# Group-norm variance on DVE behind its copy of the group sums, instead of on GpSimd

## The chip, the cores and the metric

One core of a Trainium2 chip. Time is device microseconds of one execution; a kernel's time is the median of its runs. The profile is one further execution, with the hardware profiler on. Engines: TensorE (PE; PEld is its weight load), VectorE (DVE), ScalarE (ACT), GpSimd (POOL), and SP, which issues the DMAs of the loop.

## The reference

The input is x of shape (64, 256, 14, 14), fp32. Four layers follow one another, each on all 256 channels of 196 tokens:

- L0: batch norm, depthwise 3x3 and pointwise convolution to q, k, v; k and v resized to 7x7; attention with a position bias; depthwise and pointwise convolution; residual; batch norm, relu and a 256x256 product, residual.
- L1: group norm (8 groups), linear attention with softmax over k's channels and q's tokens, projection, plus the normalised input.
- L2: group norm (32 groups), attention with 8 heads, projection, residual.
- L3: group norm (32 groups), attention with one head, projection, residual.

The part that the change touches is the group norm of L1, L2 and L3:

```python
mean = xg.mean(axis=(2, 3, 4), keepdims=True)
var = xg.var(axis=(2, 3, 4), keepdims=True)
xg = (xg - mean) * rsqrt(var + EPS)
x = xg.reshape(B, C, H, W)
return x * gamma + beta
```

## The kernel before, in words

The 64 images are worked on in 32 pairs. Channels lie on the partitions (2 blocks of 128), the tokens of both images (2 x 196) on the free axis. All weights stay on the chip.

The work of a pair is spread over several turns of one software pipeline. Each engine has a table (`PE_AT`, `ACT_AT`, `DVE_AT`, `POOL_AT`, `SP_AT`) that gives each step a start in slots, and 128 slots are one turn: slot modulo 128 is the place in the turn, slot divided by 128 says how many turns after the pair's first one the step runs. `step(t)` walks the 128 slots and issues what stands there; `run` unrolls the first and the last turns and loops over the others. So in one turn the order on each engine is fixed by its table, and steps of up to seven pairs alternate in it. Every engine's queue is worked off in that order; between engines counted semaphores (`Count`) are waited for. PSUM banks are shared by several steps in a fixed order: `full` waits until TensorE has filled a bank for a step, `free` until the steps before it have read theirs, `read` until that step has been read.

A group norm n (1, 2, 3) of a pair goes like this:

- DVE, `stats{n}`: `group_stats` takes bn_stats of 4 blocks (channel block x image), aggregates, and adds mean squared to the variance (lines 933 to 946).
- TensorE, `gn{n}`: one small product with a block matrix spreads each group's mean and mean of squares over its channels, into 8 columns of a bank (line 1414).
- DVE, `gn{n}`: copies these 8 columns to `group` in SBUF (line 1008). Ahead of it stands a wait for GpSimd's steps of the pair before.
- GpSimd, `gn{n}`: `normalized` (lines 568 to 588) works out mean squared, variance, the clamp at zero plus EPS, the power -0.5, scale, and shift, seven linked instructions of 128x4, and then applies scale and shift to the four blocks of the tile (line 587).
- ScalarE, `high{n}_c`, rounds the tile to a high part, DVE, `low{n}_c`, takes the rest as a low part (lines 781 and 1093); the products of the layer use both.

`linker` makes one instruction wait for the one before it on the same engine:

```python
def link(ins):
    done[0] += 1
    ins.then_inc(count.sem, 1)
    eng.wait_ge(count.sem, count.at(p, done[0]))
```

In one turn DVE meets the copies in the order gn2 (slot 6), gn1 (slot 45), gn3 (slot 92), each for another pair. What stands behind each copy on DVE:

- gn1: four taps of the first depthwise convolution (line 1140), then the row maximum of a head group of L2 (`nm`, line 958), which ScalarE's exponentials (line 822) need; further taps; the reciprocal of the row sums (`rden`, line 1063), which ScalarE's scaling of the heads (line 830) needs; TensorE then transposes each scaled head (line 1222). Later comes the sum of L2's projection (line 1079).
- gn2: the low part of an attention result (line 1069), low parts, the sums of L3's output `o3_1` and `o3_0` out of PSUM (line 1121), first taps and the residual sum `pw1` (line 989). `o3_0` frees bank c, which TensorE's scores of L0 (`s0_0`) fill next.
- gn3: reciprocals `rk` (line 1026) and `r` (line 1113, L3's row sums; ScalarE's line 877 needs it), the sum and maximum of `kv`, taps of the second depthwise convolution (line 1159), the maximum of another head group, and at last the residual sum `pw0` (line 989).

Of the kernel before, what the change touches and what calls it, by code (L numbers as in the profile page):

```python
# [10 lines left out]
ALU = mybir.AluOpType  # L11
# [11 lines left out]
EPS = 1e-5  # L23
# [104 lines left out]
def build(nc, a):  # L128
    ctx = ExitStack()
    with ctx:  # L130
        def sb(name, shape, dt=F32):
            return ctx.enter_context(nc.sbuf_tensor(name, shape, dt))
# [4 lines left out]
        class Count:  # L137


            def __init__(self, name, per):  # L140
                self.sem, self.per = sem(name), per
# [119 lines left out]
        class GroupNorm:  # L261


            def __init__(self, n):
                self.stats = sb(f"gn{n}_stats", [128, 4, 6])
                self.mine = sb(f"gn{n}_mine", [128, 2, 4])
                self.sq = sb(f"gn{n}_sq", [128, 4])
                self.group = sb(f"gn{n}_group", [128, 2, 4])
                self.v = sb(f"gn{n}_v", [128, 4])
                self.y = sb(f"gn{n}_y", [128, 4])  # L270
                self.t = sb(f"gn{n}_t", [128, 4])
                self.scale = sb(f"gn{n}_scale", [128, 4])
                self.shift = sb(f"gn{n}_shift", [128, 4])
                self.stat_steps = Count(f"gn{n}_stat_steps", 9)
                self.stats_ready = Count(f"gn{n}_stats_ready", 1)
                self.steps = Count(f"gn{n}_steps", 4 + 3)
                self.done = Count(f"gn{n}_done", 4)
                self.high = Count(f"gn{n}_high", KC)
                self.low = Count(f"gn{n}_low", KC)

        gn = {1: GroupNorm(1), 2: GroupNorm(2), 3: GroupNorm(3)}
# [15 lines left out]
        def tile(use):  # L297
            return home[use].t
# [4 lines left out]
        def emptied(use):  # L303
            return home[use].emptied

        def full(p, use):

            return home[use].filled, home[use].fills(p, use)
# [5 lines left out]
        def read(p, use):  # L314

            return home[use].emptied, home[use].reads(p, use, 1)
# [13 lines left out]
        def ends(*uses):  # L330

            return [use for use in uses if use == latest(*(o for o in uses if home[o] is home[use]))]
# [54 lines left out]
        def pair_of(t, u, start):  # L387

            if start % SLOTS != u:
                return None  # L390
            p = t - start // SLOTS
            return p if not isinstance(t, int) or 0 <= p < PAIRS else None

        def linker(eng, count, p, k):

            done = [k]
# [5 lines that stand above are left out]
            return link  # L402
# [9 lines left out]
        def of_image(i):  # L412
            return slice(i * TOK, (i + 1) * TOK)
# [118 lines left out]
        def _(pool):  # L532
            g = nc.gpsimd
# [7 lines left out]
            def alone():  # L541

                pool.sem_inc(pool_held, 1)
# [24 lines left out]
            def normalized(p, n, src, dst):  # L568

                t = gn[n]  # L570
                weight, bias = w[f"gn{n}_w"], w[f"gn{n}_b"]
                link = linker(pool, t.steps, p, 0)
                pool.wait_ge(*read(p, f"gn{n}"))
                pool.wait_ge(t.done.sem, t.done.at(p, 0))
                link(g.tensor_tensor(t.t[:], t.group[:, 0], t.group[:, 0], ALU.mult))  # L575
                link(g.tensor_tensor(t.v[:], t.group[:, 1], t.t[:], ALU.subtract))
                alone()
                link(g.tensor_scalar(t.v[:], t.v[:], 0.0, EPS, ALU.max, ALU.add))
                link(g.tensor_tensor(t.y[:], t.v[:], minus_half[:], ALU.pow))
                link(g.tensor_tensor(t.scale[:], t.y[:], weight[:], ALU.mult))  # L580
                link(g.tensor_tensor(t.t[:], t.group[:, 0], t.scale[:], ALU.mult))  # L581
                link(g.tensor_tensor(t.shift[:], bias[:], t.t[:], ALU.subtract))  # L582
                for c in range(KC):
                    for i in range(2):
                        j = 2 * c + i
                        alone()
                        g.tensor_scalar(dst[:, c, of_image(i)], src[:, c, of_image(i)], t.scale[:, j:j + 1],  # L587
                                        t.shift[:, j:j + 1], ALU.mult, ALU.add).then_inc(t.done.sem, 1)

            def step(t):  # L590
                for u in range(SLOTS):
# [25 lines left out]
                    if p is not None:  # L617
                        if is_first(p):
                            pool.wait_ge(weights_in, WEIGHTS)
                        if has_before(p):  # L620
                            for use in ends("out0", "out1"):
                                pool.wait_ge(*read(p - 1, use))
                        normalized(p, 1, x1, xn1)
                    p = pair_of(t, u, POOL_AT["gn2"])
                    if p is not None:
                        pool.wait_ge(gn[2].low.sem, gn[2].low.at(p, 0))
                        normalized(p, 2, x2, xn2)
# [261 lines left out]
        def _(dve):  # L889
            v = nc.vector  # L890
# [42 lines left out]
            def group_stats(p, n, src):  # L933
# [11 lines left out]
                link(v.tensor_tensor(t.sq[:], t.mine[:, 0], t.mine[:, 0], ALU.mult))  # L945
                v.tensor_tensor(t.mine[:, 1], t.mine[:, 1], t.sq[:], ALU.add).then_inc(t.stats_ready.sem, 1)

            def step(t):
                for u in range(SLOTS):

                    for g in range(GROUPS):
                        for m in range(2):
                            p = pair_of(t, u, DVE_AT[f"max{g}_{m}"])
# [8 lines left out]
                    for i in range(2):  # L962
                        use = f"s0_{i}"
                        p = pair_of(t, u, DVE_AT[use])
                        if p is not None:
# [5 lines left out]
                            link = linker(dve, l0_soft_steps[i], p, 0)  # L971
# [3 lines left out]
                        p = pair_of(t, u, DVE_AT[f"sum0_{i}"])  # L975
                        if p is not None:
                            dve.wait_ge(l0_exp_done.sem, l0_exp_done.at(p, i + 1))
                            dve.wait_ge(l0_probs.sem, l0_probs.at(p, 0))
                            link = linker(dve, l0_soft_steps[i], p, 2)
                            link(v.tensor_reduce(out=d0[:, i], in_=s0[:, i], axis=AX.X, op=ALU.add))  # L980
                            v.reciprocal(r0[:, i], d0[:, i]).then_inc(l0_soft_steps[i].sem, 1)  # L981
                    for c in range(KC):
                        use = f"pw{c}"
                        p = pair_of(t, u, DVE_AT[use])
# [5 lines left out]
                        use = f"mlp{c}"  # L990
                        p = pair_of(t, u, DVE_AT[use])
# [5 lines left out]
                    for n, src, last in ((1, x1, "mlp"), (2, x2, "out"), (3, x3, "proj")):  # L997
                        p = pair_of(t, u, DVE_AT[f"stats{n}"])
                        if p is not None:
                            for use in ends(f"{last}0", f"{last}1"):  # L1000
                                dve.wait_ge(*read(p, use))
                            group_stats(p, n, src)
                        use = f"gn{n}"
                        p = pair_of(t, u, DVE_AT[use])
                        if p is not None:
                            dve.wait_ge(*full(p, use))
                            dve.wait_ge(gn[n].steps.sem, gn[n].steps.at(p, 0))
                            v.tensor_copy(gn[n].group[:], tile(use)[:, 0:8].rearrange("p (a b) -> p a b", a=2)  # L1008
                                          ).then_inc(emptied(use), 1)

                    for j in range(4):
                        use = f"kv{j}"
                        p = pair_of(t, u, DVE_AT[use])
# [8 lines left out]
                        p = pair_of(t, u, DVE_AT[f"rk{j}"])  # L1022
# [4 lines left out]
                    for c in range(KC):  # L1027
                        use = f"q1_{c}"
                        p = pair_of(t, u, DVE_AT[use])
                        if p is not None:  # L1030

                            dve.wait_ge(*full(p, use))
                            link = linker(dve, q_less_steps, p, 2 * c)
# [4 lines left out]
                        p = pair_of(t, u, DVE_AT[f"rq{c}"])  # L1038
# [6 lines left out]
                    for c in range(KC):  # L1045
                        use = f"out{c}"
                        p = pair_of(t, u, DVE_AT[use])
# [7 lines left out]
                    for g in range(GROUPS):  # L1055
                        i = g // 2
                        for m in range(2):
                            p = pair_of(t, u, DVE_AT[f"rden{g}_{m}"])
# [6 lines left out]
                        use = f"av{g}"  # L1065
                        p = pair_of(t, u, DVE_AT[use])
# [4 lines left out]
                    for c in range(KC):  # L1071
                        use = f"proj{c}"
                        p = pair_of(t, u, DVE_AT[use])
# [8 lines left out]
                    for c in range(KC):  # L1082
                        p = pair_of(t, u, DVE_AT[f"act0_low{c}"])
# [3 lines left out]
                    for n, src, dst, _ in splits:  # L1087
                        for c in range(KC):
                            p = pair_of(t, u, DVE_AT[f"low{n}_{c}"])
# [5 lines left out]
                    for i in range(2):  # L1095
                        use = f"s3_{i}"
                        p = pair_of(t, u, DVE_AT[use])
                        if p is not None:
# [4 lines left out]
                            link = linker(dve, l3_less_steps, p, 3 * i)  # L1103
# [5 lines left out]
                        p = pair_of(t, u, DVE_AT[f"r3_{i}"])  # L1109
# [4 lines left out]
                    for i in range(2):  # L1114
                        use = f"o3_{i}"
                        p = pair_of(t, u, DVE_AT[use])
# [8 lines left out]
                    for k in range(9):  # L1125
                        p = pair_of(t, u, DVE_AT[f"conv1_{k}"])
# [17 lines left out]
                    for k in range(9):  # L1144
                        p = pair_of(t, u, DVE_AT[f"conv2_{k}"])
# [411 lines left out]
```

## Time and profile before

| what | us |
|---|---|
| median of 3 runs | 2110.89 (2110.83 to 2111.57) |
| the profiled execution, whole | 2112.12 |
| its span, first to last instruction | 2109.7 |
| TensorE busy | 2011.4 (95%), 15232 matmuls |
| TensorE weight loads busy | 1689.6 (80%) |
| ScalarE busy | 1886.4 (89%) |
| DVE busy | 1843.0 (87%) |
| GpSimd busy | 973.3 (46%) |
| DMA | 70.31 MB, mean 33 GB/s |

The mean granted TensorE clock is 0.980; it is 1.00 from 188 us on until the last 85 us. Busy times are sums of the records of an engine; records of neighbouring instructions overlap a little. A row of the timeline gives start, duration, engine, line, operation, tile written and tiles read, count where neighbouring ones are merged, and in brackets how long the engine sat idle before it and which instruction ended that. A row of the groups gives count, busy time, mean of one in ns, and the idle time before them. A row of the windows gives, for a stretch, its length and each engine's busy time with its number of instructions. Idle time of an engine that is not the bottleneck costs nothing.

### The profile page before, as it was taken

The page shows a single profiled execution, that of the slowest core. Times are in us where ns is not written, and L with a number is a line of the kernel's source. Part 1 is how long each engine was busy: PE and PEld are TensorE (multiplying, and loading weights), DVE is VectorE, ACT ScalarE, POOL GpSimd, SP SyncE. Part 2 cuts the span into 40 slices and gives each one's busy share as a digit, 9 for nine tenths or more (in the row PEclk, how much of TensorE's full clock was granted, in tenths as well). Part 3 has the DMA queues.
Part 4 walks back from the last instruction along what each step waited for, and adds up shares of the span by engine and source line. Part 5 has one row for each costly group of instructions (what it writes and reads, how often), then busy time and mean ns, then how long its engine had stood idle before and what let it go on. Part 6 is the DMA issues. An engine that isn't in the chain of part 4 may idle for free.

```text
span 2109.7 us, 57712 instructions
## 1 busy us (share of the span) xinstructions
PE 2011.4 (95%) x15232; PEld 1689.6 (80%) x15232; DVE 1843.0 (87%) x4683; ACT 1886.4 (89%) x6231; POOL 973.3 (46%) x1707
## 2 busy tenths in 40 slices
PE   4589999999999999999999999999999999999977
PEld 3367888888888888888888888888888888888766
DVE  6789999999999999999999999999999999997532
ACT  2269999999999999999999999999999999999984
POOL 3544544545444454544445454444545544453211
PEclk8799999999999999999999999999999999999988
DMA  4000011001101100110111011011101101000000
GB/s 129 16 24 24 17 40 40 24 30 38 38 23 38 38 30 24 38 38 23 38 38 36 18 38 38 23 38 38 38 15 38 38 27 34 31 32 17 24 24 39
DMA packets 29819, 70.31 MB, mean 33 GB/s; under 512 B 6252, under 2 KB 7088, under 8 KB 29744
## 3 DMA queue, kind: packets, MB, share of 16 engines
q1 hardware_dynamic: 26928, 67.68, 9.1%
q10 hardware_dynamic: 2816, 1.72, 0.3%
q8 instruction: 36, 0.59, 0.1%
q14 instruction: 39, 0.32, 0.0%
HBM read 30.85 MB, written 12.85 MB: 21 GB/s over the span
## 4 chain that ended last, share of the span: by engine, by line
PE 88%; ACT 4%; DVE 1%; issue 1%; DVEq 0%; ACTq 0%
PE ps_e L1167 21%; PE ps_c L1167 21%; PE ps_b L1167 15%; PE ps_a L1167 11%; PE ps_s L1167 10%; PE ps_s L1222 8%; ACT e L830 1%; PE ps_a L1469 1%; ACT e L822 1%; ACT pt L836 0%; PE ps_e L1298 0%; PE ps_a L1298 0%; DVE nm L958 0%; ACT e L877 0%; ACT kv L742 0%
## 5 line engine op out<-in xcount | busy, mean ns | idle before, releaser
L822 ACT ACTIVATE e<-ps_s,nm 98x196 f32<-98x196 f32 x1024 | 423.9, 436 | 36.2 <-DVE nm L958 32.0
L830 ACT ACTIVATE e<-e,rden 98x196 f32<-98x196 f32 x1024 | 403.2, 462 | 0.2 <-DVE rden L1063 0.2
L1159 DVE SCALAR_TENSOR_TENSOR y<-opad,w_dw,y 128x406 f32<-128x406 f32 x512 | 314.9, 666 | 0.0
L1140 DVE SCALAR_TENSOR_TENSOR y<-xpad,w_dw,y 128x406 f32<-128x406 f32 x512 | 298.4, 636 | 0.0
L587 POOL TENSOR_SCALAR xn<-x,gn_scale,gn_shift 128x196 f32<-128x196 f32 x384 | 286.1, 757 | 20.8 <-POOL gn_shift L582 20.8
L575 POOL TENSOR_TENSOR gn_t<-gn_group 128x4 f32<-128x4 f32 x96 | 27.7, 289 | 563.7 <-DVE gn_group L1008 430.1
L958 DVE TENSOR_REDUCE nm<-ps_s 98x4 f32<-98x784 f32 x256 | 239.4, 966 | 34.2 <-PE ps_s L1167 34.2
L836 ACT COPY pt<-ps_s 98x392 f32<-98x392 f32 x512 | 233.3, 502 | 4.7 <-PE ps_s L1222 2.8
L1222 PE MATMUL ps_s<-w_eye,e 98*98 98x98 f32 x2048 | 228.9, 249 | 7.3 <-ACT e L830 7.2
L1222 PEld LDWEIGHTS ps_s<-w_eye,e 98*98 98x98 f32 x2048 | 200.5, 130 | 38.8 <-issue 22.3
L822 ACT ACTIVATION_READ_ACCUMULATOR e<-ps_s,nm 98x1 f32 x1024 | 222.7, 217 | 0.0
L599 POOL TENSOR_TENSOR p<-s,r 98x392 f32<-98x392 f32 x64 | 64.3, 1005 | 225.5 <-DVE r L981 225.5
L1167 PE MATMUL ps_c<-xs,ws_q 128*128 128x392 f32 x768 | 166.8, 352 | 0.0
L1167 PEld LDWEIGHTS ps_c<-xs,ws_q 128*128 128x128 f32 x768 | 133.0, 189 | 0.1
L1093 DVE TENSOR_TENSOR xs<-xn,xs 128x392 fp32r<-128x392 f32 x192 | 115.6, 603 | 16.8 <-ACT xs L781 15.4
L581 POOL TENSOR_TENSOR gn_t<-gn_group,gn_scale 128x4 f32<-128x4 f32 x96 | 123.3, 1285 | 7.5
L1167 PE MATMUL ps_s<-k,q 32*98 32x196 f32 x2048 | 118.6, 345 | 8.3 <-ACT q L791 2.3
L1167 PE MATMUL ps_s<-pt,v 98*32 98x196 f32 x2048 | 112.5, 337 | 6.8 <-ACT e L822 6.3
L1167 PEld LDWEIGHTS ps_s<-k,q 32*98 32x98 f32 x2048 | 77.4, 160 | 49.3 <-issue 28.0
L1167 PE MATMUL ps_a<-ws_v,xs 128*98 128x256 f32 (+1 forms) x768 | 112.3, 288 | 0.9 <-ACT opad L721 0.7
L1167 PEld LDWEIGHTS ps_a<-ws_v,xs 128*98 128x98 f32 x768 | 94.6, 163 | 21.6 <-issue 10.3
L939 DVE BATCH_NORM_STATS2 gn_stats<-x 128x6 f32<-128x196 f32 x384 | 109.7, 347 | 1.1
(223 smaller groups left out, 5326.6 us busy)
## 6 DMA issues: line engine op xcount, KB each, us to landing
x_in<-in_x SPq DMA_DIRECT2D x32, 392.0 KB, 3.2
x_res<-in_x SPq DMA_DIRECT2D x32, 392.0 KB, 3.1
x2b<-x SPq DMA_DIRECT2D x32, 392.0 KB, 2.7
out<-x SPq DMA_DIRECT2D x32, 392.0 KB, 2.6
out_pairs<-out SPq DMA_DIRECT2D x32, 392.0 KB, 2.5
w_q<-in_q SPq DMA_DIRECT2D x3, 256.0 KB
w_k<-in_k SPq DMA_DIRECT2D x3, 256.0 KB
w_v<-in_v SPq DMA_DIRECT2D x3, 256.0 KB
```

The lines of the kernel that those rows point to most:

```text
L581: link(g.tensor_tensor(t.t[:], t.group[:, 0], t.scale[:], ALU.mult))
L587: g.tensor_scalar(dst[:, c, of_image(i)], src[:, c, of_image(i)], t.scale[:, j:j + 1], t.shift[:, j:j + 1], ALU.mult, ALU.add).then_inc(t. ...
L822: s.activation(e2[:, j, tc], tile(use)[0:HALF, of_image(tc)], ACT.Exp, bias=nm2[:, j, tc:tc + 1], accum_out=den2[:, 2 * i + tc, h:h + 1]). ...
L830: s.activation(e2[:, j, tc], e2[:, j, tc], ACT.Copy, scale=rden2[:, 2 * i + tc, h:h + 1]).then_inc(p2_done[j].sem, 1)
L836: s.copy(turned(j), tile(use)[0:HALF, 0:N2]).then_inc(emptied(use), 1)
L939: v.bn_stats(t.stats[:, j], src[:, j // 2, of_image(j % 2)]).then_inc(t.stat_steps.sem, 1)
L958: v.tensor_reduce(out=nm2[:, two], in_=ps_s[0:HALF, two, 0:N2].rearrange("p b (c n) -> p b c n", c=2), axis=AX.X, op=ALU.max, negate=True) ...
L1093: v.tensor_tensor(dst[:, 1, c], src[:, c], dst[:, 0, c], ALU.subtract).then_inc(gn[n].low.sem, 1)
L1140: v.scalar_tensor_tensor(out=dst, in0=window(xpad, c, k, CR), scalar=tap, in1=dst, op0=ALU.mult, op1=ALU.add).then_inc(conv1_steps.sem, 1)
L1159: v.scalar_tensor_tensor(out=dst, in0=window(opad, c, k, CR), scalar=tap, in1=dst, op0=ALU.mult, op1=ALU.add).then_inc(conv2_steps.sem, 1)
L1167: return nc.tensor.matmul(dst, lhsT, rhs, start=start, stop=stop)
L1222: last = nc.tensor.transpose(tile(use)[0:HALF, of_tile(sc, tc)], e2[:, j, tc, sc * HALF:(sc + 1) * HALF], eye[0:HALF, 0:HALF])
```

## The change

Three of the seven small instructions of `normalized` go from GpSimd to DVE: mean squared, the subtraction, and the clamp with EPS. A new function `variance` on DVE issues the copy, waits for it, and issues the three, each linked to the one before by a new counter `var_steps`. Mean squared goes to `sq`, which the statistics use before. GpSimd waits for the third count of `var_steps` instead of for the copy, and starts with the power. Power, scale, shift and the four passes over the tile stay on GpSimd; the counter `steps` has four steps a pair instead of seven. The tables of slots stay as they are.

```diff
-                self.steps = Count(f"gn{n}_steps", 4 + 3)
+                self.steps = Count(f"gn{n}_steps", 1 + 3)
+                self.var_steps = Count(f"gn{n}_var_steps", 3)
...
-                pool.wait_ge(*read(p, f"gn{n}"))
+                pool.wait_ge(t.var_steps.sem, t.var_steps.at(p, 3))
                 pool.wait_ge(t.done.sem, t.done.at(p, 0))
-                link(g.tensor_tensor(t.t[:], t.group[:, 0], t.group[:, 0], ALU.mult))
-                link(g.tensor_tensor(t.v[:], t.group[:, 1], t.t[:], ALU.subtract))
-                alone()
-                link(g.tensor_scalar(t.v[:], t.v[:], 0.0, EPS, ALU.max, ALU.add))
                 link(g.tensor_tensor(t.y[:], t.v[:], minus_half[:], ALU.pow))
...
+            def variance(p, n, use):
+
+                t = gn[n]
+                link = linker(dve, t.var_steps, p, 0)
+                v.tensor_copy(t.group[:], tile(use)[:, 0:8].rearrange("p (a b) -> p a b", a=2)).then_inc(emptied(use), 1)
+                dve.wait_ge(*read(p, use))
+                link(v.tensor_tensor(t.sq[:], t.group[:, 0], t.group[:, 0], ALU.mult))
+                link(v.tensor_tensor(t.v[:], t.group[:, 1], t.sq[:], ALU.subtract))
+                v.tensor_scalar(t.v[:], t.v[:], 0.0, EPS, ALU.max, ALU.add).then_inc(t.var_steps.sem, 1)
...
                             dve.wait_ge(gn[n].steps.sem, gn[n].steps.at(p, 0))
-                            v.tensor_copy(gn[n].group[:], tile(use)[:, 0:8].rearrange("p (a b) -> p a b", a=2)
-                                          ).then_inc(emptied(use), 1)
+                            variance(p, n, use)
```

## Rows read from the trace of the kernel before

**Rows 1.** The page, chain that ended last, shares of the span by engine

```profile
PE 88%; ACT 4%; DVE 1%; issue 1%; DVEq 0%; ACTq 0%
```

**Rows 2.** Windows: us, busy of PE, PEld, DVE, ACT, POOL; clock, DMA, GB/s

```profile
257.00:318.50 61.50, 61.47 (x479) 51.96 (x476) 57.04 (x146) 58.72 (x197) 30.88 (x54) 1.00 0.10 35
318.50:1606.60 1288.10, 1285.60 (x9955) 1087.72 (x9956) 1200.60 (x3046) 1230.21 (x4076) 637.59 (x1114) 1.00 0.09 33
1606.60:1913.00 306.40, 305.90 (x2370) 258.94 (x2370) 279.40 (x715) 291.71 (x969) 149.71 (x269) 1.00 0.09 31
```

**Rows 3.** Groups of instructions by line and shape, GpSimd, whole span

```profile
L576 POOL TENSOR_TENSOR gn_v<-gn_group,gn_t 128x4 f32<-128x4 f32 x96 | 33.2, 345 | 7.5
L578 POOL TENSOR_SCALAR gn_v<-gn_v 128x4 f32<-128x4 f32 x96 | 28.3, 294 | 19.2 <-POOL gn_v L576 19.2
L575 POOL TENSOR_TENSOR gn_t<-gn_group 128x4 f32<-128x4 f32 x96 | 27.7, 289 | 563.7 <-DVE gn_group L1008 430.1 <-issue 133.7
```

**Rows 4.** Timeline of GpSimd, a first normalisation in the loop

```profile
1047.39 0.47 POOL L575 TENSOR_TENSOR gn_t<-gn_group 128x4 f32<-128x4 f32 x1 [0.81 <-DVE gn_group L1008]
...
1049.10 1.25 POOL L579 TENSOR_TENSOR gn_y<-gn_v,minus_half 128x4 f32<-128x4 f32 x1
```

**Rows 5.** Timeline of ScalarE, pair 0 and the last pair

```profile
95.23 0.52 ACT L781 CAST xs<-xn 128x392 fp32r<-128x392 f32 x1 [0.76 <-POOL xn L587]
...
2083.45 0.52 ACT L781 CAST xs<-xn 128x392 fp32r<-128x392 f32 x1 [1.81 <-POOL xn L587]
```

**Rows 6.** Timeline of DVE around a first normalisation in the loop

```profile
1045.60 0.16 DVE L945 TENSOR_TENSOR gn_sq<-gn_mine 128x4 f32<-128x4 f32 x1
1045.80 0.16 DVE L946 TENSOR_TENSOR gn_mine<-gn_mine,gn_sq 128x4 f32<-128x4 f32 x1
1047.06 0.17 DVE L1008 COPY gn_group<-ps_a 128x8 f32<-128x8 f32 x1 [1.09 <-PE ps_a L1167]
1047.15 2.30 DVE L1140 SCALAR_TENSOR_TENSOR y<-xpad,w_dw,y 128x406 f32<-128x406 f32 x4
1049.63 1.86 DVE L958 TENSOR_REDUCE nm<-ps_s 98x4 f32<-98x784 f32 x2 [0.17 <-PE ps_s L1167]
...
1055.78 0.17 DVE L1063 RECIPROCAL rden<-den 98x4 f32<-98x4 f32 x1
...
1060.90 0.63 DVE L1079 SCALAR_TENSOR_TENSOR x<-ps_e,pb,x2b 128x392 f32<-128x392 f32 x1 [0.23 <-PE ps_e L1167]
```

**Rows 7.** Timeline of DVE, behind a second normalisation in the loop

```profile
1032.12 0.74 DVE L1121 SCALAR_TENSOR_TENSOR out<-ps_c,ob,out 128x196 f32<-128x196 f32 x2
```

**Rows 8.** Groups of instructions by line and shape, DVE, whole span

```profile
L1036 DVE TENSOR_SCALAR bq_less<-nmq,w_qb 128x2 f32<-128x2 f32 x64 | 19.0, 297 | 2.3
...
L894 DVE TENSOR_SCALAR bn_half<-bn_v 128x4 f32<-128x4 f32 x1 | 0.2, 170 | 0.0
```

**Rows 9.** Timeline of ScalarE, scaling of the heads behind rows 6

```profile
1055.98 1.50 ACT L830 ACTIVATE e<-e,rden 98x196 f32<-98x196 f32 x4
...
1057.86 0.81 ACT L830 ACTIVATE e<-e,rden 98x196 f32<-98x196 f32 x2
```

**Rows 10.** Timeline of TensorE, the two steps that need these results

```profile
1033.50 0.93 PE L1167 MATMUL ps_c<-k,q 128*98 128x98 f32 x8
...
1058.74 0.84 PE L1222 MATMUL ps_s<-w_eye,e 98*98 98x98 f32 x8
```

**Rows 11.** Timeline of DVE, the wait ahead of the pointwise sum

```profile
1027.84 0.57 DVE L989 TENSOR_TENSOR x<-ps_c,x_res 128x392 f32<-128x392 f32 x1 [0.75 <-PE ps_c L1167]
```

**Rows 12.** Timeline of DVE, behind pair 1's first normalisation

```profile
137.56 1.85 DVE L958 TENSOR_REDUCE nm<-ps_s 98x4 f32<-98x784 f32 x2 [0.22 <-PE ps_s L1167]
```

**Rows 13.** Timeline of ScalarE, behind the first third-normalisation

```profile
224.07 0.42 ACT L822 ACTIVATE e<-ps_s,nm 98x196 f32<-98x196 f32 x1 [0.59 <-DVE nm L958]
...
227.98 0.32 ACT L843 CAST as<-ps_s 128x196 fp32r<-128x196 f32 x1 [0.18 <-PE ps_s L1167]
```

**Rows 14.** Timeline of ScalarE, behind the last third-normalisation

```profile
2079.31 0.81 ACT L877 ACTIVATE e<-e,r 98x196 f32<-98x196 f32 x2 [2.55 <-DVE r L1113]
```

## Prediction

> **What bounds the kernel now.** I read the chain that ended last first: it is TensorE for 88% of the span [rows 1]. The question is then how much TensorE idles where. The windows answer it: over 21 pairs of the loop (1288.10 us, so 61.34 us a pair) TensorE is busy 1285.60 us [rows 2]. It waits 0.12 us a pair. In the loop nothing that ends earlier on GpSimd or DVE can shorten the run; something that ends later on DVE can lengthen it. The stretches from 257 us and up to 1913 us are as full [rows 2], so TensorE fills (1913 - 257)/61.34 = 27 pairs. Ahead of them the pipeline fills and behind them it empties; there the engines wait for each other.
>
> **What leaves GpSimd.** Three instructions per normalisation, 96 of each: 27.7 + 33.2 + 28.3 = 89 us of busy time [rows 3]. On the path from DVE's copy to the power this is, in the first normalisation of a pair, 1047.39 to 1049.10 = 1.71 us [rows 4]. GpSimd is busy for half of the loop (637.59 of 1288.10 us) [rows 2], so the busy time itself is worth nothing; only the earlier end of the normalised tile could be, where someone waits for it. ScalarE shows such waits twice: 0.76 us for pair 0, 1.81 us for the last pair [rows 5].
>
> **What comes to DVE.** Three linked small instructions behind the copy, each started only when the one before has finished. The nearest row is the same pattern in the statistics: 1045.60 to 1045.80, 0.20 us from start to start with a record of 0.16 [rows 6]. Unlinked, the next instruction starts 0.09 us after the copy (1047.06 to 1047.15) [rows 6]. So copy to multiply 0.20, to subtract 0.20, to the tensor_scalar 0.20, and 0.09 to the next, against 0.09 before: everything behind the copy on DVE starts **0.60 us later**. The last instruction has immediate scalars; the kernel has one such of 0.170 us, and one with pointer scalars and fewer columns of 0.297 us [rows 8]. Bounds: below, 3 x 0.09 = 0.27 us if the waits cost nothing; above, 0.60 + 0.13 = 0.73 us if the tensor_scalar is as slow as the second. I take 0.60, since the 0.20 is the same operation, shape and link. GpSimd's power then starts 0.60 + 0.17 + 0.16 = 0.93 us after the copy instead of 2.04 (1047.06 to 1049.10).
>
> The Trainium skill (VectorE: DVE Perf Modes, section "The DRAIN you can't avoid") says that a semaphore after each of several chained DVE instructions costs nothing against one after the last. By it the sum would be +0.3 us instead of +2.0; the 0.20 against 0.09 us [rows 6] speaks against it.
>
> The wait on GpSimd moves from the copy to the third step; behind it on GpSimd's queue are the power, scale, shift and the four passes of the tile, and ScalarE's splits wait for those. The wait ahead of DVE's copy, for GpSimd's steps of the pair before, is about a pair old and free. No DMA is issued, moved or passed by.
>
> **Where 0.60 us on DVE goes in the loop**, normalisation by normalisation. "Slack" is the start of the waiting instruction minus the end of what it needs, less 0.03 us for the signal (rden ends 1055.95, ScalarE starts 1055.98) [rows 6, 9].
> - First (copy at 1047.06). Behind it are four taps, then a maximum that already waits 0.17 us for TensorE [rows 6]; records overlap by 0.08, so 0.25 is absorbed and 0.35 goes on to rden at 1055.78 and so to ScalarE at 1055.98. ScalarE's third head ends at 1057.86 + 0.81 = 1058.67 [rows 9]; its transposes are the second half of the eight from 1058.74 on (0.84 us), so they start at about 1058.74 + 0.42 = 1059.16, or 1059.08 where records overlap by the same 0.08 [rows 10]. Slack 0.38: it holds, by 0.03 us. What remains on DVE is taken up before the projection's sum, which waits 0.23 us for TensorE [rows 6].
> - Second. The last sum of o3_0 ends at 1032.12 + 0.74 = 1032.86 and frees the bank that TensorE writes from 1033.50 [rows 7, 10]: slack 0.61, and between copy and sum (some 4 us) DVE waits for nobody. 0.60 uses it up.
> - Third. Its hold-up ends at latest where DVE waits 0.75 us for the pointwise sum [rows 11]; I see no TensorE work that needs an earlier one of these within 0.2 us.
> Since two of three places are left with 0.01 to 0.03 us, I put 0.02 us a pair: 27 x 0.02 = 0.5 us.
>
> **At the edges** ScalarE and DVE set the pace, so a hold-up there is on the path. Pair 1's first normalisation stands before a maximum that waits 0.22 us [rows 12]: 0.60 - 0.30 = 0.30 us; pair 2's repeats it: 0.30. At the first third-normalisation DVE is behind: ScalarE waits 0.59 us for its maximum, and then has only a 0.18 us wait for TensorE to give back [rows 13]: 0.60 - 0.26 = 0.34. In the last third-normalisation the reciprocal r stands right behind the copy and ScalarE has waited 2.55 us for it [rows 14], with TensorE idle behind: 0.60. For pair 0 I count nothing: GpSimd is earlier, DVE later. Sum of the edges 1.54 us.
>
> **Sum**: 0.5 + 1.5 = +2.0 us. The profiled execution took 2112.12 us, so 2114.1; the median of the runs stands 1.2 us under it, 2110.89, so **2112.9 us**, +0.1%. About 0.2% (4.2 us) is what a measurement of this kernel can tell from no change.
>
> **Rivals.**
> 1. *A wait of TensorE in every pair* (slower). Place: the bank freed by o3_0's sum, and the third head's transposes. It decides from a hold-up of 0.61 us on. Price at 0.73: 0.12 + (0.48 - 0.38) = 0.22 us x 27 = 5.9 us, and edges 2 x 0.43 + 0.47 + 0.73 = 2.1: 2118.9 us. For: the slack is used up to the hundredth, and the ends of matmuls are modelled. Against: 0.20 a step is a measured pattern in the same loop. Chance 0.22.
> 2. *The links are free.* Each of the three steps takes 0.09 us, the hold-up is 0.27: nothing in the loop, at the edges 0 + 0 + 0.01 + 0.27: +0.3, 2111.2 us. For: the unlinked step of 0.09 us; against: the linked one of 0.20, both in one stretch [rows 6]. Chance 0.13. This is the case that the Trainium skill's section named above describes.
> 3. *The earlier tile pays* (faster). Each of ScalarE's two waits for GpSimd ends at most 2.04 - 0.93 = 1.1 us earlier: -2.2 us, 2108.7, if DVE's low halves and TensorE's older work didn't end last there. In the loop at most the 0.12 us a pair could go, -3.2 us. Only both together, 2105.5, pass 0.2%. Against: TensorE's loop is full without a wait for GpSimd. Chance 0.05.
> 4. *The change makes nothing of its own*: DVE's steps vanish in waits everywhere, 2110.9. Chance 0.04; the row of 2.55 us, with r right behind, speaks against it.
> The forecast keeps 0.56.
>
> **Numbers.** The forecast, rivals 2 and 4 and parts of 3 and 1 (hold-ups of 0.61 to 0.65 us) lie within 0.2%: 0.56 + 0.13 + 0.04 + 0.03 + 0.02 = 0.78. Slower: the other 0.20 of rival 1. Faster: the other 0.02 of rival 3. The range runs from 2110.0 (rival 4, less a microsecond of scatter) to 2118.0, which takes in rival 1 up to a hold-up of about 0.71 us; it leaves out rival 3 and the top of rival 1, together 0.15 or so.
>
> **What would show it.** Each step right: multiply, subtract and tensor_scalar on DVE at 0.20 us start to start, the next instruction 0.68 us after the copy; GpSimd's busy time down by some 89 us and DVE's up by 96 x 3 x 0.165 = 47 us; the power 0.93 us after the copy; TensorE's pair still 61.3 to 61.4 us; the maximum after the first normalisation without its 0.17 us wait; r at the end 0.60 us later. Wrong: a pair of 61.5 us or more, with new waits of TensorE for o3_0's sum or for ScalarE's scaling; or a last chain in which GpSimd's passes appear.

## The result, and the profile after

The changed kernel takes **2161.62 us** (median of 4 runs, 2160.23 to 2162.25), the kernel before 2110.86 beside it: ratio 1.0239 [1.0226, 1.0252], slower by 50.8 us. The forecast was 2112.9, its range ended at 2118.0. The profiled execution took 2160.23 us, its span is 2158.2 (2109.7 before).

The page of the changed kernel: its busy times, two of its DMA queues, and the chain that ended last.

```profile
PE 2030.6 (94%) x15232; PEld 1690.4 (78%) x15232; DVE 1885.1 (87%) x4971; ACT 1890.8 (88%) x6231; POOL 827.7 (38%) x1419
...
q14 instruction: 154, 1.26, 0.2%
q8 instruction: 37, 0.61, 0.1%
...
PE 58%; DVE 18%; issue 11%; ACT 5%; DVEq 2%; ACTq 0%
```

What was moved is there: DVE has 288 instructions and 42 us more (1843.0 before), GpSimd 146 us less (973.3 before). But the chain, TensorE's for 88% before [rows 1], is now DVE's for 18% and "issue" for 11%. And q14, a queue that carries instructions (an edit of DVE's program alone will move its packets below, so DVE's are among them), has 154 packets; before it had 39 (0.32 MB, so 8.2 KB each). From 450 to 1800 us, deep in the loop, it carried none before and 106 after. That is new work that stands in no term of the forecast.

The waits of DVE say where it hurts (us in total, times, longest):

```profile
DVE x L1058 <- issue: 42.3, 23, 2.0
```

The loop has 24 turns (t = 7 to 30), so it branches back 23 times. L1058 (L1052 before) is the projection's sum x2, whose two halves stand on either side of the branch. Before there is no idle time between them:

```profile
1023.93 0.62 DVE L1052 SCALAR_TENSOR_TENSOR x<-ps_e,w_pb,xn 128x392 f32<-128x392 f32 x1
1024.47 0.62 DVE L1052 SCALAR_TENSOR_TENSOR x<-ps_b,w_pb,xn 128x392 f32<-128x392 f32 x1
```

The changed kernel's DVE around the branch and behind a first normalisation, then GpSimd (start, us, operation, idle time before it and what ended that):

```profile
1043.83 0.62 DVE L1058 SCALAR_TENSOR_TENSOR x<-ps_e,w_pb,xn 128x392 f32<-128x392 f32 x1
1046.20 0.62 DVE L1058 SCALAR_TENSOR_TENSOR x<-ps_b,w_pb,xn 128x392 f32<-128x392 f32 x1 [1.75 <-issue]
...
1068.29 0.17 DVE L949 COPY gn_group<-ps_a 128x8 f32<-128x8 f32 x1 [1.22 <-PE ps_a L1173]
1068.49 0.16 DVE L951 TENSOR_TENSOR gn_sq<-gn_group 128x4 f32<-128x4 f32 x1
1068.69 0.16 DVE L952 TENSOR_TENSOR gn_v<-gn_group,gn_sq 128x4 f32<-128x4 f32 x1
1068.89 0.17 DVE L953 TENSOR_SCALAR gn_v<-gn_v 128x4 f32<-128x4 f32 x1
1068.98 2.29 DVE L1146 SCALAR_TENSOR_TENSOR y<-xpad,w_dw,y 128x406 f32<-128x406 f32 x4
...
1069.22 1.30 POOL L576 TENSOR_TENSOR gn_y<-gn_v,minus_half 128x4 f32<-128x4 f32 x1 [1.35 <-DVE gn_v L953]
```

The three new steps stand 0.20 us apart, as their model in [rows 6], the next instruction 0.69 us behind the copy, and the power 0.93 us behind it. What TensorE waits for from 413.4 to 1635.8 us, where nothing of the kind is listed for the kernel before:

```profile
PE ps_e L1173 <- DVE gn_mine L943: 17.2, 20, 1.0
PE ps_c L1173 <- DVE kv L1024: 5.2, 19, 0.3
PE ps_e L1173 <- DVE x L1085: 4.5, 19, 0.3
```

The window of that stretch (columns as in [rows 2]): TensorE is idle for 28.5 of 1222.4 us.

```profile
413.40:1635.80 1222.40, 1193.87 (x9153) 999.24 (x9153) 1127.31 (x2975) 1134.20 (x3738) 494.70 (x846) 1.00 0.09 33
```

The largest wait, 0.9 us a pair, stands right behind the gap: the group sums of the second normalisation need the statistics that DVE does after the branch. The period of a pair comes from two starts of the first normalisation's statistics, 22 pairs apart: (1825.81 - 431.68)/22 = **63.37 us**, against 61.34.

```profile
431.68 1.14 DVE L936 BATCH_NORM_STATS2 gn_stats<-x 128x6 f32<-128x196 f32 x4
...
1825.81 1.14 DVE L936 BATCH_NORM_STATS2 gn_stats<-x 128x6 f32<-128x196 f32 x4
```

### The profile page after: what moved, and what is told of

Read it like the earlier page. It is cut to its first block, busy times and chain, and to the rows that moved or that the text cites. A ratio compares the mean times of both kernels' runs of the same rounds, so it can differ in the third digit from the quotient of the medians.

```text
span 2158.2 us, 57568 instructions
## 1 busy us (share of the span) xinstructions
PE 2030.6 (94%) x15232; PEld 1690.4 (78%) x15232; DVE 1885.1 (87%) x4971; ACT 1890.8 (88%) x6231; POOL 827.7 (38%) x1419
## 4 chain that ended last, share of the span: by engine, by line
PE 58%; DVE 18%; issue 11%; ACT 5%; DVEq 2%; ACTq 0%
PE ps_e L1173 15%; PE ps_c L1173 14%; PE ps_b L1173 9%; PE ps_s L1173 7%; PE ps_a L1173 6%; PE ps_s L1228 5%; DVE y L1146 4%; DVE y L1165 3%; DVE nm L965 3%; ACT e L827 1%; DVE m L1110 1%; ACT e L819 1%; DVE kv L1024 1%; DVE x L1085 1%; DVE x L1058 1%
## 5 line engine op out<-in xcount | busy, mean ns | idle before, releaser
L827 ACT ACTIVATE e<-e,rden 98x196 f32<-98x196 f32 x1024 | 409.1, 469 | 29.6 <-DVE rden L1069 29.5
L576 POOL TENSOR_TENSOR gn_y<-gn_v,minus_half 128x4 f32<-128x4 f32 x96 | 105.7, 1101 | 681.0 <-DVE gn_v L953 532.4
L584 POOL TENSOR_SCALAR xn<-x,gn_scale,gn_shift 128x196 f32<-128x196 f32 x384 | 334.3, 883 | 20.6 <-POOL gn_shift L579 20.6
L1165 DVE SCALAR_TENSOR_TENSOR y<-opad,w_dw,y 128x406 f32<-128x406 f32 x512 | 321.2, 677 | 0.0
L1228 PE MATMUL ps_s<-w_eye,e 98*98 98x98 f32 x2048 | 234.3, 250 | 6.8 <-ACT e L827 6.2
L819 ACT ACTIVATION_READ_ACCUMULATOR e<-ps_s,nm 98x1 f32 x1024 | 230.1, 225 | 0.0
L1099 DVE TENSOR_TENSOR xs<-xn,xs 128x392 fp32r<-128x392 f32 x192 | 111.0, 579 | 15.4 <-ACT xs L778 13.5
L1173 PE MATMUL ps_e<-ws_kv,xs 128*98 128x512 f32 x384 | 105.7, 410 | 9.7 <-DVE x L1085 5.7
```

The source lines that it names most:

```text
L819: s.activation(e2[:, j, tc], tile(use)[0:HALF, of_image(tc)], ACT.Exp, bias=nm2[:, j, tc:tc + 1], accum_out=den2[:, 2 * i + tc, h:h + 1]). ...
L827: s.activation(e2[:, j, tc], e2[:, j, tc], ACT.Copy, scale=rden2[:, 2 * i + tc, h:h + 1]).then_inc(p2_done[j].sem, 1)
L1099: v.tensor_tensor(dst[:, 1, c], src[:, c], dst[:, 0, c], ALU.subtract).then_inc(gn[n].low.sem, 1)
L1165: v.scalar_tensor_tensor(out=dst, in0=window(opad, c, k, CR), scalar=tap, in1=dst, op0=ALU.mult, op1=ALU.add).then_inc(conv2_steps.sem, 1)
L1173: return nc.tensor.matmul(dst, lhsT, rhs, start=start, stop=stop)
L1228: last = nc.tensor.transpose(tile(use)[0:HALF, of_tile(sc, tc)], e2[:, j, tc, sc * HALF:(sc + 1) * HALF], eye[0:HALF, 0:HALF])
```

## Experiments: code loading

**Theory A**: DVE's code for one turn of the loop is 333 instructions in the compiled program before, and 349 after. If it lies over one more block of DVE's instruction buffer than the buffer can keep, each turn loads its code again and the branch waits for it. The packets of one turn of the changed kernel, found with narrow windows of the DMA view, come at 1044.1 and 1046.7 (around the branch), 1054.1, 1080.7 and 1101.9 us; DVE's timeline laid against the compiled program puts the last three near instructions 65, 193 and 321 of the turn (an estimate, give or take 6), 128 apart. A shift of the whole loop would then do the same harm or good as its length, without a variance anywhere. The rivals in the expectations: A2, the length alone decides; B, the code has no part in it, and the linked operations are what costs. The edit of these runs is two lines at the very start of DVE's program, with N = 16, 32, 60 and 128 for the kernel before and 80 for the changed one:

```diff
+            for _ in range(N):
+                dve.sem_inc(dve_held, 1)
             dve.wait_ge(first_in, FIRST)
```

**Before, shifted by 60.**

> The kernel before, with 60 extra semaphore increments (on a semaphore that nobody waits for) at the very start of VectorE's program, where VectorE waits 6.7 us for its first transfer anyway; its loop keeps its 333 instructions and no norm's variance is moved. Theory A (code loading by place: the changed kernel's extra instructions move VectorE's loop across one more block of its instruction buffer, and every turn then loads code again): as slow as the changed kernel, 2155 to 2165 us, with instruction packets in all turns of the loop, some 5 a turn, and a gap of some 1.8 us on VectorE at each turn. Theory A2 (code loading by length alone: 349 instructions are too many, 333 are not): 2111 us, no packets in the loop. Theory B (the three linked operations hold VectorE up, and the code has no part in it): 2111 us.

Measured: 2141.09 us, 1.0141 [1.0124, 1.0158]. The instruction queue carries as much as in the changed kernel, 109 of its packets from 450 to 1800 us. The queue, and DVE's wait at the branch (whole span):

```profile
q14 instruction: 154, 1.26, 0.2%
...
DVE x L1054 <- issue: 41.9, 23, 2.0
```

TensorE's, from 412.8 to 1621.8 us:

```profile
PE ps_e L1169 <- DVE gn_mine L948: 22.0, 20, 1.3
```

Nothing in the loop was edited, and yet the packets, the 23 gaps and the wait of TensorE are those of the changed kernel. A2 and B can't make that. The time, 30 us more, is less than A said: loading is not the whole of the 50.8.

**Changed kernel, shifted by 80.**

> The changed kernel, with 80 extra semaphore increments at the very start of VectorE's program; its loop keeps its 349 instructions with all three variances on VectorE. Theory A: the loop lies within as many blocks as that of the kernel before, no instruction packets in its turns, no gap at the turn, and the time is that of the hold-up alone, 2111 to 2115 us. Theories A2 and B: 2158 to 2165 us, as the changed kernel without them.

Measured: 2131.09 us, 1.0095 [1.008, 1.0109]; 39 instruction packets, none from 450 to 1800 us, no gap at the branch.

```profile
q14 instruction: 39, 0.32, 0.0%
```

So with all 349 instructions in place the loading is gone (A2 falls), but 20 us stay, where A expected the forecast's 2. Two costs, then: some 30 us of loading and 20 us of something else, which is B or a rival of it.

**Before, shifted by 16, 32 and 128.**

> The kernel before with 16 extra semaphore increments at the start of VectorE's program. Theory A, with block bounds placed by the packet times of the changed kernel's turn (estimate: room for 24 more, give or take 6): the loop still fits, 2111 us. A2 and B: 2111 us. Were the increments themselves what costs, this run would show some of it.

> The kernel before with 32 extra semaphore increments at the start of VectorE's program. Theory A, with the same estimate (room for 24, give or take 6): the loop no longer fits, 2155 to 2165 us with packets in every turn. A2 and B: 2111 us.

> The kernel before with 128 increments at the start of VectorE's program. Theory A with blocks of 128 instructions (the 8 KB of one instruction packet at 64 bytes an instruction): a shift of one whole block changes nothing, no packets in the loop, 2110 to 2113 us. A with larger blocks, or any cost of the increments themselves: packets in every turn or more time, 2130 us or above.

Measured: by 16, 2111.07 us, 1.0002 [0.9993, 1.0011], 39 packets; by 128, 2111.72 us, 1.0003 [0.9994, 1.0012], 39 packets; by 32, 2210.11 us, 1.0473 [1.0455, 1.0492], 154 packets. The packets at 32 are what A said, the time is 45 us above its range. Increments cost nothing that can be told; nor does a whole block of 128; and the kernel before lay between 16 and 31 instructions short of the bound. By the estimate above the loop stays loaded where it lies in three blocks, and not where it lies in four. Each turn then brings five packets: 106 in (1800 - 450)/63.37 = 21.3 turns. Five where the loop lies in four blocks would mean that one more is fetched ahead, and that four (4 x 8.2 KB is some 33 KB) are held at a time; that is an estimate, which no run tested.

The Trainium skill (Runtime: NRT & Kernel Launch, section "Instruction fetch mechanics") says the same in kind: the code streams in ahead, and a taken branch to a block that is no longer held stalls for its load. Its sizes, 256 instructions a block and two blocks, are not those seen here: packets of 8.2 KB, a shift of 128 without effect, and a loop of 333 that stays. The measurement decides.

**What made 32 so dear.** It was 69 us worse than 60. The gap on DVE in a turn of that run, the wait of TensorE behind it, and windows of half a microsecond (the column after POOL is TensorE's granted clock):

```profile
1070.23 0.63 DVE L1054 SCALAR_TENSOR_TENSOR x<-ps_b,w_pb,xn 128x392 f32<-128x392 f32 x1 [2.83 <-issue]
...
1072.92 0.39 PE L1169 MATMUL ps_e<-gn_mine,w_group 128*128 128x8 f32 x2 [2.10 <-DVE gn_mine L948]
...
1072.50:1073.00 0.50, 0.08 (x1) 0.09 (x1) 0.33 (x2) 0.50 (x2) 0.00 (x0) 1.00 0.00 0
1073.00:1073.50 0.50, 0.50 (x6) 0.50 (x7) 0.49 (x2) 0.50 (x2) 0.00 (x0) 1.00 0.00 0
1073.50:1074.00 0.50, 0.50 (x7) 0.50 (x5) 0.50 (x4) 0.50 (x3) 0.18 (x1) 0.83 0.00 0
1074.00:1074.50 0.50, 0.50 (x4) 0.50 (x4) 0.50 (x2) 0.50 (x2) 0.41 (x2) 0.50 0.00 0
...
1076.50:1077.00 0.50, 0.50 (x3) 0.50 (x3) 0.40 (x1) 0.50 (x2) 0.46 (x1) 0.50 0.00 0
1077.00:1077.50 0.50, 0.50 (x4) 0.50 (x3) 0.08 (x1) 0.50 (x2) 0.25 (x2) 0.75 0.00 0
```

Its gap on DVE is longer (2.83 us), TensorE waits 2.10, and then runs at half its clock (the 1.2 GHz level) for some 3.5 us. Behind the changed kernel's wait of 0.73 us the clock stayed at 1.00. An estimate from these rows: TensorE's wait is some 0.95 us a turn longer than at 60 (38.9 us in 19 times, against 22.0 in 20), and 3.5 us at half clock cost 1.75; 23 x 2.7 is 62 of the 69 us. Why the gap is longer was tested with a shift of 44:

> The kernel before, shifted by 44. Shifted by 32 it took 2210 us with a gap of 2.83 us on VectorE at each turn, shifted by 60 2141 us with one of 1.96 us. Theory Q: at 32 the last piece of the loop is so short (estimate: 8 instructions) that the block behind the loop is requested just ahead of the branch, and the branch's own block queues behind it; at 44 the last piece has some 20 instructions, the request is over by the branch: gap 1.8 to 2.0 us, 2137 to 2145 us, TensorE's clock whole in the loop. Rival: the gap grows with what stands ahead of the first block border (68 instructions at 32, 41 at 60), and 44 lies halfway: 2165 to 2185 us.

Measured: 2150.96 us, 1.0189 [1.0172, 1.0206]; DVE's gap is 42.2 us in 23 times, 1.83 each, and the clock is 1.00 from 413.4 to 1635.8 us. The gap is what theory Q said, the time is 6 us above its range and 14 below the rival's. The excess over the shift of 60 goes with a second, small gap, 9.4 us in 24 times ahead of the reciprocal r (L1115), and a TensorE wait of 0.3 us behind it for the projection's sum x3 (L1081); the changed kernel has both (7.5 us in 24 times; the third row of its TensorE waits). Theory Q fits: at 32 two packets follow each other within half a microsecond where the gap begins (1067.0 and 1067.5; it begins at 1067.4), at 60 they are 6 us apart (1093.0 and 1099.4). That the second queues behind the first was not shown by itself.

## Experiments: the hold-up

What are the 20 us of the shifted changed kernel? Its period is 62.08 us, 0.74 more than before, in every pair, and TensorE has a listed wait for kv (413.4 to 1635.8 us):

```profile
PE ps_c L1175 <- DVE kv L1026: 5.2, 19, 0.3
```

**Theory H**: it is the 0.60 us by which DVE is held behind each copy. All runs here are shifted by as much as keeps their loops loaded (39 or 40 packets), but for the last.

**Before, with three spare steps on DVE**, GpSimd as it was:

```diff
                             v.tensor_copy(t.group[:], ...).then_inc(emptied(use), 1)
+                dve.wait_ge(*read(p, use))
+                link(v.tensor_tensor(t.sq[:], t.group[:, 0], t.group[:, 0], ALU.mult))
+                link(v.tensor_tensor(t.spare[:], t.group[:, 1], t.sq[:], ALU.subtract))
+                v.tensor_scalar(t.spare[:], t.spare[:], 0.0, EPS, ALU.max, ALU.add).then_inc(...)
```

> The kernel before, whose GpSimd still works the variance out, with three more linked operations of the same kind on VectorE behind each copy of the group sums; they write a tile that nobody reads. 80 increments at the start of VectorE's program keep its loop (350 instructions) within its buffer, as in the run of the changed kernel so shifted, which took 2131 us. Theory H (the 20 us that are left are the hold-up of 0.60 us of VectorE behind each copy): 2128 to 2134 us, again a wait of TensorE for kv and some 0.75 us more a pair. Rival G (they come from GpSimd's side: the normalised tile is ready earlier and its passes meet other work): 2111 to 2113 us.

Measured: 2129.17 us, 1.009 [1.007, 1.0109]; period 62.0 us; the same wait of TensorE for kv.

```profile
PE ps_c L1180 <- DVE kv L1031: 5.2, 19, 0.3
```

With GpSimd as it was, 18 of the 20 us come back, and 0.66 of the 0.74 us a pair. GpSimd's side has no part that can be told from the scatter.

**Changed kernel, steps spread**: multiply, subtract and clamp stand 2, 4 and 7 slots behind the copy (first norm), 2, 5 and 7 (second), 2, 4 and 5 (third), each with its own wait:

```diff
             def variance(p, n, use):
...
                 v.tensor_copy(t.group[:], ...).then_inc(emptied(use), 1)
-                dve.wait_ge(*read(p, use))
-                link(v.tensor_tensor(t.sq[:], t.group[:, 0], t.group[:, 0], ALU.mult))
-                link(v.tensor_tensor(t.v[:], t.group[:, 1], t.sq[:], ALU.subtract))
-                v.tensor_scalar(t.v[:], t.v[:], 0.0, EPS, ALU.max, ALU.add).then_inc(t.var_steps.sem, 1)
...
                             variance(p, n, use)
+                        for k, later in enumerate({1: (2, 4, 7), 2: (2, 5, 7), 3: (2, 4, 5)}[n]):
+                            p = pair_of(t, u, DVE_AT[use] + later)
+                            if p is not None:
+                                variance_step(p, n, use, k)
```

> The changed kernel, shifted by 80 increments, with the three operations of each variance spread among VectorE's next instructions, so that each link is over before it is waited for: the hold-up behind the copy is 3 x 0.09 = 0.27 us in pieces instead of 0.60 us at once, with the same number of operations. Theory H: at each of the three places the delay falls under what the next step has to spare; 2110 to 2116 us. Rival T (what costs is the time of three more operations, or the work on GpSimd, not the waits of the links): 2125 to 2131 us.

Measured: 2112.60 us, 1.0007 [0.9998, 1.0016]; period 61.34 us, and TensorE waits for nobody in the list; it is idle for 0.07 of 1222.40 us, where it was for 8.0 in the run that was shifted but not spread:

```profile
413.40:1635.80 1222.40, 1222.33 (x9458) 1033.54 (x9457) 1148.01 (x3074) 1170.10 (x3866) 528.69 (x880) 1.00 0.09 33
```

The same operations, with the links' waits filled, cost nothing that can be told: Rival T falls.

**Two steps on DVE**, the clamp on GpSimd:

```diff
-                link(v.tensor_tensor(t.v[:], t.group[:, 1], t.sq[:], ALU.subtract))
-                v.tensor_scalar(t.v[:], t.v[:], 0.0, EPS, ALU.max, ALU.add).then_inc(t.var_steps.sem, 1)
+                v.tensor_tensor(t.v[:], t.group[:, 1], t.sq[:], ALU.subtract).then_inc(t.var_steps.sem, 1)
...
+                link(g.tensor_scalar(t.v[:], t.v[:], 0.0, EPS, ALU.max, ALU.add))
                 link(g.tensor_tensor(t.y[:], t.v[:], minus_half[:], ALU.pow))
```

> The changed kernel, shifted likewise (loop of 342 instructions), with only multiply and subtract on VectorE; the clamp with the epsilon goes back to GpSimd. The hold-up is 0.40 us behind each copy. Theory H with a threshold (only what exceeds the slack counts: some 0.32 us reach ScalarE at the first norm against 0.38 to spare, 0.40 against 0.61 at the second, 0.28 - 0.20 = 0.08 us at the third): 2112 to 2117 us. Theory H in proportion (each 0.20 us costs a third of 20 us): 2124 us.

Measured: 2115.24 us, 1.0021 [1.0012, 1.0029]; period 61.45. Two thirds of the hold-up cost a fifth of the 20 us: a threshold, not a proportion. TensorE is late at the bank of kv alone, by 0.32 us (1.38 us behind the kernel before ahead of it, 1.70 at it), and gets 0.19 back by the next scores.

**Spread, but not shifted**:

> The changed kernel with its variances spread as before, but without the 80 increments: its loop of 349 instructions lies where that of the changed kernel lies. If code loading and hold-up are two costs that add, loading alone is left here, as in the kernel before shifted by 60: 2139 to 2145 us, packets in every turn, a gap of some 1.8 us at the turn. If the two only cost together, or the hold-up causes the loading: 2112 us.

Measured: 2146.27 us, 1.0165 [1.0148, 1.0182]; 154 packets, DVE's gap 42.1 us in 23 times. Loading alone costs 34 us at this place, a little above what was expected; with the hold-up it is 50.8. The two are separate and nearly add up (34 + 20 = 54).

## Why the prediction was wrong, point by point

**No term for the code.** This is the step that cost most: 30 to 34 of the 50.8 us, by the runs where loading stands alone. "What comes to DVE" counted three instructions' time and waits, not where their code lies, and "No DMA is issued, moved or passed by" left out the instruction queue, which moved 106 packets more from 450 to 1800 us. Loading was put at nothing, without a reason. Three operations with their register steps and waits are 16 more instructions in the loop, and the unrolled pairs ahead of it are 36 longer (1016 against 980 in the compiled program), which alone goes past the 16 to 31 that were left. The profile of before shows the risk: its instruction queue has packets while pairs are unrolled and none from 450 to 1800 us. Periods of 62.67 us (shifted by 60) and 62.79 (spread, unshifted) are 1.33 and 1.45 over 61.34; times 23 branches, 31 and 33 us. None of the four rivals is this one.

**The hold-up's size was right, what lay under it was not.** The 0.60 us were met to 0.01. The second step that failed is "Since two of three places are left with 0.01 to 0.03 us, I put 0.02 us a pair": it is 0.74, 20 us in all. The rows of the shifted changed kernel place by place, where lines are without loading (its turns stand 7.58 to 8.02 us behind those of before at these points):

```profile
1054.81 0.17 DVE L951 COPY gn_group<-ps_a 128x8 f32<-128x8 f32 x1 [1.21 <-PE ps_a L1175]
...
1055.51 2.30 DVE L1148 SCALAR_TENSOR_TENSOR y<-xpad,w_dw,y 128x406 f32<-128x406 f32 x4
1057.72 1.85 DVE L967 TENSOR_REDUCE nm<-ps_s 98x4 f32<-98x784 f32 x2
...
1062.79 1.34 DVE L1148 SCALAR_TENSOR_TENSOR y<-xpad,w_dw,y 128x406 f32<-128x406 f32 x2
1064.05 0.17 DVE L1071 RECIPROCAL rden<-den 98x4 f32<-98x4 f32 x1
...
1064.25 1.51 ACT L827 ACTIVATE e<-e,rden 98x196 f32<-98x196 f32 x4 [0.25 <-DVE rden L1071]
...
1066.13 0.81 ACT L827 ACTIVATE e<-e,rden 98x196 f32<-98x196 f32 x2
...
1040.30 0.74 DVE L1129 SCALAR_TENSOR_TENSOR out<-ps_c,ob,out 128x196 f32<-128x196 f32 x2
...
1041.27 0.93 PE L1175 MATMUL ps_c<-k,q 128*98 128x98 f32 x8
...
1080.36 0.67 DVE L1026 TENSOR_TENSOR kv<-ps_c,w_kvb 98x512 f32<-98x512 f32 x1
...
1081.09 1.35 PE L1175 MATMUL ps_c<-xs,ws_q 128*128 128x392 f32 x6 [0.28 <-DVE kv L1026]
```

- First normalisation: the maximum has lost its wait of 0.17 us, and goes 0.34 us later, as the forecast had it. But the two taps ahead of rden take 1.34 us, not 1.18 (why, no run shows), and rden comes 0.52 us later (1055.78 to 1064.05, 7.75 behind), not 0.35. That is 0.14 more than the 0.38 us to spare; TensorE is 0.26 us later behind it (1060.80 to 1068.82). The rest lies in the signal: the third head ends at 1066.13 + 0.81 = 1066.94 and its transposes start at 1067.08, 0.14 us later, where 0.03 were set aside.
- Second: the sum of o3_0 ends at 1041.04 and TensorE writes the bank at 1041.27. The 0.03 us set aside for a signal is 0.23 here, so the slack of 0.61 was 0.41: 0.19 us later (1033.50 to 1041.27, 7.58 behind).
- Third: "I see no TensorE work that needs an earlier one of these within 0.2 us" was an oversight, and the dearest of the three. The fourth kv sum is the third instruction behind the copy, and TensorE writes its bank next. These two rows of the kernel before would have shown it: it ends at 1072.42 and TensorE writes its bank at 1072.57.

```profile
1071.75 0.67 DVE L1018 TENSOR_TENSOR kv<-ps_c,w_kvb 98x512 f32<-98x512 f32 x1
...
1072.57 1.32 PE L1167 MATMUL ps_c<-xs,ws_q 128*128 128x392 f32 x6
```

0.15 us to spare against a hold-up of 0.60: TensorE is 0.50 us later (8.52 behind instead of 8.02). Of that 0.20 comes back by the next scores of a group, which start at 1079.84 and 1088.17, 8.33 apart.

Sum: 0.26 + 0.19 + 0.50 - 0.20 = 0.75 us a pair, times 27 is 20 us. With the loading of the unshifted loop the period is 2.03 us longer: 23 x 2.03 + 4 x 0.74 for the full pairs outside the loop + the forecast's 1.5 at the edges = 51 us, against 50.8 measured.

**The rivals.** Rival 1 had the right mechanism, at two of the three places, but made it begin at a hold-up of 0.61 us; it begins below 0.40, where a pair is already 0.11 us longer, all of it at the third place. At the third place it stood in neither the forecast nor a rival. Rival 2 falls: each linked step starts 0.20 us behind the one before, not 0.09. The Trainium skill's sentence on a semaphore after each of several chained instructions (VectorE: DVE Perf Modes, "The DRAIN you can't avoid") is not borne out by these steps of 128x4; spreading them, which fills the links, takes 18.5 us off. Rival 3 is not seen: the power starts 1.1 us earlier, but the run is not faster for it than the one in which GpSimd kept its work (2131.09 and 2129.17 us).

**The edges** held in the one row that can be set beside the forecast: the last reciprocal r comes late by what was said. In the changed kernel ScalarE has waited 3.13 us for it, 2.55 before [rows 14]. The 0.94 us at the front can't be read from a trace: by the loop the kernel before and the same kernel shifted by 128, which takes as long in all, are further apart (430.76 and 428.21 us, for the same statistics).

```profile
2127.86 0.81 ACT L874 ACTIVATE e<-e,r 98x196 f32<-98x196 f32 x2 [3.13 <-DVE r L1119]
```

## What to carry to other kernels

Where an engine's work runs in a real loop, look at the instruction queue inside it: no packets meant here that the loop stayed loaded, and a few more instructions, in the loop or ahead of it, ended that; some harmless increments ahead of the loop moved it back. When the bounding engine has no idle time, take every bank that the delayed engine frees in the next few microseconds, one by one, and compare its end with the next write; "I see none" is not a slack. And three linked small operations cost the waits of their links, which other work can fill: spread among it, they cost nothing that could be measured here.

## What had not been expected

- A shift of 32 instructions ahead of a loop that is itself unchanged made the kernel 99 us slower, one of 16 or 128 nothing.
- TensorE's granted clock fell from 1.00 to 0.50 shortly after a wait of 2.10 us and stayed there for some 3.5 us, and did not fall behind waits of 0.73 us, nor, where the loop was shifted by 60 or 44, behind waits of up to 1.3 us (1.00 from 413.4 to 1635.8 us in both).
- GpSimd's busy time fell by 146 us where three groups of 89 us left [rows 3]: its multiply of mean and scale took 123.3 us before (1285 ns each) and 30.6 after (319 ns each), while the passes of the tile went from 757 to 883 ns. Why was not tried; GpSimd does not bound this kernel.
- None of the runs beats the kernel before; the best with the variance on DVE, the spread steps at a shifted place, can't be told from it.
